# Two blocks of the first adjacency row multiply x and x2 as they arrive, and two chunks of a graph kernel take their blocks in another order

## The reference, cut to what matters

```python
h  = relu(adj @ x @ gcn_w + gcn_b)            # product 1: adj @ x
h  = layernorm(h) * ln_g + ln_b
y  = mamba(h)                                 # conv of 4 taps, silu, a scan over the 4096 rows, gate
x1 = layernorm(x + y)
def conv(v, W, b):                            # products 2 and 3: adj @ x1, adj @ x2
    ax = adj @ v
    t = ax + (1.0 + eps) * ax
    for i in range(3):
        t = relu(t @ W[i].T + b[i])
    return t
out = layernorm(x1 + concat(conv(x1, W1, b1), conv(x2, W2, b2)) @ Wm.T + bm)
```

## Time and profile before

| what | value |
|---|---|
| three executions | 809.51, 811.18, 810.60 us, median 810.6 |
| the profiled execution, its time | 809.39 us |
| its span, first to last instruction | 807.6 us |
| TensorE busy | 792.5 us (98%) |
| VectorE, GpSimd, ScalarE busy | 626.0, 620.3, 437.8 us |
| DMA | 227.42 MB, mean 282 GB/s |
| granted TensorE clock, mean | 0.998 |

### The profile page before, as it was taken

How to read it: one execution, slowest core, us unless ns; L and a number is a source line. 1 busy time by engine, 2 the same in 40 slices (tenths; PEclk the granted TensorE clock), 3 DMA queues, 4 the chain that set the end, 5 groups by cost and what they waited for, 6 DMA issues and landing times.

```text
span 807.6 us, 7621 instructions
## 1 busy us (share of the span) xinstructions
PE 792.5 (98%) x2094; PEld 362.8 (45%) x2094; DVE 626.0 (78%) x881; ACT 437.8 (54%) x822; POOL 620.3 (77%) x300
## 2 busy tenths in 40 slices
PE   7999999999999999999999999999999999999996
PEld 3434444444454444443444444434544454444453
DVE  0146799999898988889899898977988988882136
ACT  0166676477647764766477646662486545321234
POOL 0005899999998989889989998979799899970036
PEclk9999999999999999999999999999999999999999
DMA  9999777777766999998779966899878897887602
GB/s 340 393 367 326 239 225 269 229 254 239 240 226 210 372 375 328 343 375 329 240 254 354 393 244 210 292 329 337 283 248 274 313 338 244 309 295 272 248 26 79
DMA packets 63390, 227.42 MB, mean 282 GB/s; under 512 B 7394, under 2 KB 8180, under 8 KB 44916
## 3 DMA queue, kind: packets, MB, share of 16 engines
q1 hardware_dynamic: 24804, 156.40, 52.0%
q10 hardware_dynamic: 38544, 70.54, 27.5%
HBM read 224.29 MB, written 2.62 MB: 281 GB/s over the span
## 4 chain that ended last, share of the span: by engine, by line
PE 88%; DVE 4%; DMA 3%; ACT 3%; issue 1%; ACTq 0%; DVEq 0%
PE p_x L503 47%; PE p_x L533 16%; PE p_two L533 11%; PE p_m L604 2%; DMA x_s<-x_tiles 2%; PE p_dA L696 2%; PE p_m L620 2%; DMA spread_C<-bc_rows 1%; DVE p_h L980 1%; PE p_two L594 1%; PE p_m L587 1%; PE p_m L624 1%; PE p_two L581 1%; PE p_h L696 1%; PE p_m L616 1%; DVE prod L993 1%
## 5 line engine op out<-in xcount | busy, mean ns | idle before, releaser
L503 PE MATMUL p_x<-ring,x_s 128*128 128x512 f32 x1024 | 455.8, 596 | 2.8 <-DMA x_s<-x_tiles 2.6
L1214 POOL TENSOR_TENSOR bh<-spread,dtu 128x1024 f32<-128x1024 f32 x127 | 299.7, 2360 | 34.2 <-DVE bh L1157 34.2
L1223 POOL TENSOR_TENSOR y<-y,prod 128x1024 f32<-128x1024 f32 x120 | 282.6, 2355 | 54.1 <-DVE prod L993 46.0
L503 PEld LDWEIGHTS p_x<-ring,x_s 128*128 128x128 f32 x1024 | 192.7, 191 | 249.0 <-issue 241.6
L980 DVE TENSOR_TENSOR_SCAN p_h<-p_dA,state,bh 128x512 f32<-128x512 f32 x224 | 276.1, 1278 | 20.7 <-ACT p_dA L706 9.7
L706 ACT ACTIVATE p_dA<-dt,A 128x512 f32<-128x512 f32 x256 | 172.0, 686 | 128.4 <-DVE p_h L980 126.8
L993 DVE TENSOR_TENSOR prod<-p_h,spread_C 128x1024 f32<-128x1024 f32 x120 | 145.7, 1214 | 1.4 <-DMA spread_C<-bc_rows 0.2
L533 PE MATMUL p_x<-ring,x 128*128 128x512 f32 x304 | 137.3, 593 | 0.8 <-ACT acc L939 0.8
L533 PE MATMUL p_two<-ring,x 128*128 128x512 f32 x208 | 94.3, 594 | 2.1 <-DVE dtu L1093 2.0
L533 PEld LDWEIGHTS p_x<-ring,x 128*128 128x128 f32 x304 | 57.1, 190 | 70.8 <-issue 70.8
L424 POOL TENSOR_SCALAR dtu<-prod,mv,rstd 128x128 f32<-128x128 f32 x26 | 20.4, 802 | 63.0 <-ACT rstd L965 63.0
(11 more groups left out here) (133 smaller groups left out, 605.4 us busy)
## 6 DMA issues: line engine op xcount, KB each, us to landing
ring<-adj_blocks SPq DMA_DIRECT2D x143, 1024.0 KB, 7.1
spread_C<-bc_rows ACTq DMA_DIRECT2D x128, 256.0 KB, 5.8
spread<-bc_rows ACTq DMA_DIRECT2D x127, 256.0 KB, 5.1
ring<-adj_blocks SPq DMA_DIRECT2D x8, 256.0 KB, 7.1
x_s<-x_tiles SPq DMA_DIRECT2D x8, 256.0 KB, 10.4
x_s<-x_tiles ACTq DMA_DIRECT2D x7, 256.0 KB, 9.8
out_tiles<-dtu SPq DMA_DIRECT2D x7, 256.0 KB, 2.0
pack<-pack_w ACTq DMA_DIRECT2D x1, 1026.0 KB, 11.8
```

What stands on the lines that cost most here:

```text
L503: return pe.matmul(bank[:, :], tiles[:, JT * m + jt, :], ring[:, i % RING, jt, :], start=opens, stop=closes)
L1214: pool.tensor_tensor(bh[:, i % 3, :, :], both(spread[:, q, :]), dtu[:, c % 2, :, :], ALU.mult).then_inc(s_bmul, 1)
L1223: pool.tensor_tensor(y[:, c % 2, :, :], y[:, c % 2, :, :], prod[:, i % 2, :, :], ALU.add).then_inc(s_acc, 1)
```

## The change

- BOTH = 2: the blocks (0, 0) and (0, 1) multiply x and x2 as they come in the start. The blocks' partial sum for x2 closes in `p_x2`, VectorE copies it to `kept` (a slice of x1's last buffer, unused until chunk 4 is over), and adds it when the rest of row 0 is complete, in a step of its own (`rows_0`) that takes the place of ScalarE's copy of that row. ScalarE's queue brings the first 8 tiles of x2 between those of x. PIECES is 1: only block 0 comes in pieces.
- The two blocks are used for x1 alone later, at the end of chunk 3: eight matmuls of x2 are gone from that chunk and stand in the start.
- In chunk 5 the block (5, 4) comes before the x2 blocks (5, 5) to (5, 7), the sum of row 2 opens after (5, 5), and rows 3 and 4 change places: row 3 now gathers in `p_x` behind row 2, row 4 in `p_two`, last.
- FILL: 11 matmuls instead of 10 stand behind the first gcn and 11 instead of 12 behind the first dt.

```diff
-PIECES = 2
+PIECES = 1
+BOTH = 2
-RAMP = row(X, 0, ALL)
+RAMP = row(ONE, 0, ALL[:BOTH]) + row(X, 0, ALL[BOTH:])
-FILL = {"gcn": 10, "in_x": 7, "x_proj": 3, "dt": 12}
+FILL = {"gcn": 11, "in_x": 7, "x_proj": 3, "dt": 11}
 CHUNK_BLOCKS = [
...
-    row(X, 6, (1,)) + row(X1, 4, (0, 1)) + mixed(row(X, 6, ALL[2:]), row(X2, 0, ALL[3:])) + row(DOUBLE, 0, ALL[:3]),
+    row(X, 6, (1,)) + row(X1, 4, (0, 1)) + mixed(row(X, 6, ALL[2:]), row(X2, 0, ALL[3:])) + row(DOUBLE, 0, (2,))
+    + row(X1, 0, (0, 1)),
...
-    row(DOUBLE, 5, ALL[:4]) + row(X2, 5, (5, 6)) + row(DOUBLE, 5, (4,)) + row(X2, 5, (7,))
-    + row(X1, 2, (2, 3, 4)) + row(X1, 4, (2, 3, 4)) + row(X1, 3, (2, 3, 4)),
+    row(DOUBLE, 5, ALL[:5]) + row(X2, 5, (5,)) + row(X1, 2, (2, 3, 4)) + row(X2, 5, (6, 7))
+    + row(X1, 3, (2, 3, 4)) + row(X1, 4, (2, 3, 4)),
 SUMS = [
...
-        ("x", 5, (0, 1, 2, 3, 4)), ("x", 2, (2, 3, 4)), ("two", 4, (2, 3, 4)), ("x", 3, (2, 3, 4)),
+        ("x", 5, (0, 1, 2, 3, 4)), ("x", 2, (2, 3, 4)), ("x", 3, (2, 3, 4)), ("two", 4, (2, 3, 4)),
...
+        kept = x1[:, KEEP - 1, :, :].rearrange("p t n -> p (t n)")
...
+                if part == "x2" and i < BOTH:
+                    opens, closes = (i, jt) == (0, 0), (i, jt) == (BOTH - 1, JT - 1)
...
+            for jt in range(JT):
+                pe.wait_ge(s_tile[jt], 48 if jt < 2 else 16)
+                block_part(0, jt, jt + 1)
+                block_part(0, JT + jt, JT + jt + 1)
...
+            for jt, tiles in ((0, slice(0, 1)), (1, slice(1, JT))):
+                act.dma_start(x_s[:, tiles, :], x_d[0, :, tiles]).then_inc(s_tile[jt], 16)
+                act.dma_start(x2_s[:, tiles, :], x2_d[0, :, tiles]).then_inc(s_tile[jt], 16)
...
+                elif name == "rows_0":
+                    dve.tensor_tensor(ax2[:, q % 2, :], p_x2[:, :], kept, ALU.add).then_inc(s_ax2, 1)
...
+            dve.wait_ge(s_blk_used, BOTH)
+            dve.tensor_copy(kept, p_x2[:, :]).then_inc(s_kept, 1)
```

More of the change, by code:

```diff
@@ L131, in blocks_with @@
     return [i for i, blk in enumerate(LOADS) if part in blk[0] and blk[1] == n]
-FIRST_OF = {(part, n): blocks_with(part, n)[0] for part in ("x", "x2") for n in range(NC)}
+FIRST_OF = {(part, n): blocks_with(part, n)[BOTH if (part, n) == ("x2", 0) else 0]
+            for part in ("x", "x2") for n in range(NC)}
 LAST_OF = {(part, n): blocks_with(part, n)[-1] for part in ("x", "x2") for n in range(NC)}
@@ L471, in _ @@
                 load(NBLK + k)
+                if k < BOTH:
+                    continue
                 sp_.dma_start(x2_s[:, JT * k:JT * (k + 1), :], x2_d[k]).then_inc(s_x2s[k], 16)
@@ L500, in first @@
                     wait(pe, s_taken, taken)
-                if part == "x2" and jt == 0 and i < FIRST[1]:
+                    if part == "x2" and taken == 0:
+                        pe.wait_ge(s_kept, 1)
+                if part == "x2" and i < BOTH:
+                    opens, closes = (i, jt) == (0, 0), (i, jt) == (BOTH - 1, JT - 1)
+                if part == "x2" and jt == 0 and PIECES <= i < FIRST[1] and m:
                     pe.wait_ge(s_x2s[m], 16)
@@ L631, in _ @@
                 pe.matmul(p_m[:, 0:WARM_W], sq[:, 0:P], sq[:, 0:WARM_W], start=True, stop=True)
-            for k in range(NBLK):
-                if k:
-                    pe.wait_ge(s_xs[k], 16)
-                if k < PIECES:
-                    for jt in range(JT):
-                        pe.wait_ge(s_tile[JT * k + jt], 32 if k == 0 and jt < 2 else 16)
-                        block_part(k, jt, jt + 1)
-                else:
-                    block_part(k, 0, JT)
+            for jt in range(JT):
+                pe.wait_ge(s_tile[jt], 48 if jt < 2 else 16)
+                block_part(0, jt, jt + 1)
+                block_part(0, JT + jt, JT + jt + 1)
+            for k in range(1, NBLK):
+                pe.wait_ge(s_xs[k], 16)
+                block_part(k, 0, len(block_steps(LOADS[k])))
             pe.wait_ge(s_pack, 16)
@@ L945, in _ @@
                             take_x(n)
-                        if rows_complete(n, "x2") == (c, unit):
+                        if n and rows_complete(n, "x2") == (c, unit):
                             take_x2(n)
@@ L1100, in step @@
                     aggregate(s_stats, b).then_inc(s_stats, 1)
+                elif name == "rows_0":
+                    q = X2_ROWS.index(0)
+                    dve.wait_ge(s_px2, 1 + X2_DOUBLE.index(0))
+                    dve.wait_ge(s_mm2, 4 * (q - 2) + 1)
+                    dve.tensor_tensor(ax2[:, q % 2, :], p_x2[:, :], kept, ALU.add).then_inc(s_ax2, 1)
                 elif name == "mlp3":
@@ L1123, in steps_of @@
                     put(min(unit + 1, S - 1), int(unit == S - 1), "mlp3", q)
+                done = rows_complete(0, "x2")
+                if c == done[0]:
+                    put(done[1] + 1, 0, "rows_0", 0)
                 if c + 1 < NC:
```

16 lines of the change are left out of this document (7 added, 9 removed).

## The result

The changed kernel takes **816.4 us** (median of 6 runs, 813.95 to 816.8) for 810.5 us of the kernel before (6 runs, 808.17 to 812.15). The ratio is 1.007, with a 95% interval of 1.0048 to 1.0093: 0.7% slower. The profiled execution took 816.80 us, its span is 815.0 us; before they were 809.39 and 807.6.

A forecast was written before the change was run, and what follows sets the result against it. TensorE, busy 98% of the span, was taken as the bound. Terms +5.8 - 1.0 - 2.2 + 1.9 = +4.5 us gave 815.1 us; the terms' bounds were 812.6 to 818, the range 810.9 to 818.5.

The forecast's parts named there:

- TensorE is the bound, and only its gaps change the time: Whole kernel: TensorE busy 98% of the span, its 768 matmuls stay, all gaps together some 7 us.
- The start: Row 0: 6.9 us of x2 work added, 3.3 us of gaps removed; done at 41.8, +5.8 us (+4.7 to +7.1).
- the nearest neighbour's 7.1 us after issue: Start: landing time of the third DMA (256 KB), taken for the fourth, issued at 2.1, so landing at 9.2.
- The filling: Chunk 0: eleventh matmul fills the 0.5 us before in_x, and the 0.2 us ring wait goes; -1.0 us.
- Chunks 1 and 2: Chunks 0 to 2 move by +4.8 as a whole, the scan with them, locked to TensorE's steps.
- Chunk 3: Eight matmuls and the dtu wait go, 7.9 us, but only -2.2 us is gained (-3.2 to -1.3).
- the scan gains only what it waits for TensorE: Chunk 3: VectorE's waits for out (0.93) and mlp3 (1.64) less rows_0 (0.69) give 1.9 us; with rounding, 1.8.
- the four new waits: Chunk 3: the other 5.7 us become TensorE waits ahead of x_proj, dt, mlp0 and z.
- Chunk 5: New wait for ScalarE's copy against two removed waits, 2.3 us: balance +1.9 us (+1 to +2.5).
- The forecast's wait of 4.2 us: Chunk 5: TensorE waits from 519.73 to 523.9 for ScalarE's copy of row 5's sum, behind table load and decays.
- rival 4: Chunk 5's gap makes the granted clock fall; four matmuls at 1.72 us add 3.4 us, 818.5 us; chance 0.10.
- Rivals 1 to 3: Rival 1 all hidden, 803.3 us (0.10); rival 2 chunk 5 smooth, 810.9 (0.12); rival 3 chunk 3 follows, 809.4 (0.08).

The follow-up runs named there:

- the one with zero weights: Changed kernel with four zero-weight matmuls of 512 columns added where TensorE waits for ScalarE's copy in chunk 5; 814.3 us, ratio 1.0061.
- the two with the reordered start: Changed kernel with row 0's x steps of block 0 ahead of its x2 steps, 817.3 us; the same start together with both moves, 816.4 us.
- both moves: Changed kernel, old chunk 5, reordered start, x2 block moved from chunk 4 to 3, row 5's x1 block from 5 to 4; 816.4 us, ratio 1.0078.

## Why the prediction was right, and where its terms were off

The forecast was 815.1 us (+4.5) with slower as the likeliest; the medians gave 816.4 (+5.9). In the profiles the terms add up to +7.4: three came out larger by 1.1 to 1.4 us and one smaller by 1.1, so part of the agreement is that misses cancelled. (The lower bound that follows from the forecast's terms is 812.1 us, not 812.6.)

- **TensorE is the bound, and only its gaps change the time.** Right: its records are the same in number, and every us of the difference is found as a gap or as records at double spacing.
- **The start, +5.8, measured +6.93** (and +7.0 to +7.6 in the four other kernels with this very start: the upper bound of 7.1 was too low). In the changed kernel the mechanism was right, the second piece waits for the DMA issued fourth. The size was off by its landing: I took the nearest neighbour's 7.1 us after issue, 9.2; it started at 10.25, 8.1 us after the issue at 2.14. That 1.05 us is nearly the whole miss of 1.1. The neighbour came from a kernel in which the second block was in pieces with packets of 2 KB, and here its packets were of 8 KB. In the four other kernels the DMA landed at 9.6 to 10.4, and in two of them (the one with zero weights, the one with a block moved to chunk 3) TensorE didn't wait for it at all: its records still stood 0.85 us apart when it landed, until 11.8 and 10.7, and row 0 was done at +7.63 and +7.04. So the slow beginning was a second mechanism, which the forecast didn't have. The forecast also rested on a wrong reading of the earlier trace rows: I counted 3.3 us of gaps in the old start as time spent waiting for x that work could fill. About 2 us of it were four records at double spacing (1.0, 1.0, 1.0 and 0.85 us apart), which no transfer explains and which the new start has as well.
- **The filling, -1.0, measured -0.86** in the changed kernel; alone in the kernel before it was worth nothing, since the ring's wait and chunk 3 took it back.
- **Chunks 1 and 2, forecast 0, measured +1.35** in this profile: a wait of 0.7 us for ScalarE's copy `ax`, which stood behind a DMA issue of its own, and smaller ones. Of the four other kernels with this very start three show none of it and the one with the old chunk 5 has 1.06, in chunk 2; the two with the reordered start have 1.35 and 0.8. It comes in some executions and not in others, and what decides that stays open.
- **Chunk 3, -2.2 (-3.2 to -1.3), measured -3.3.** The step "the scan gains only what it waits for TensorE" held, and 6.9 us less work made the chunk 3.0 to 4.0 us shorter in five profiles. Mis-sized was what VectorE gains, 3.0 us for 1.8 here. A third wait for TensorE went, 0.30 us ahead of gcn's first step, and one of 0.49 us between a scan and its own copy; and rows_0 made its stretch only 0.4 us longer and not 0.69 (from the scan's start to the copy of its state 2.96 us, for 2.57 at the same place before). The wait for the rows of C gave nothing here (1.41 us for 1.23), but it is what varies most from one profile to the next (0 to 3.6 us), and the range didn't count it. Of the four new waits three came (x_proj 0.86, dt 1.13, z 1.12); the one ahead of mlp0 came in other kernels with the same chunk (2.0 us in the kernel with zero weights in chunk 5, 1.4 us in the one with the old chunk 5). ScalarE's copy at the chunk's end is where TensorE waits, and VectorE's scan is what it waits for.
- **Chunk 5, +1.9, measured +3.3.** The forecast's wait of 4.2 us was 4.0 with the 0.16 us added to its bracket, and without the fall of the clock the term is +1.94 (the run with zero weights): the term was right. What came on top is the mechanism of rival 4, the granted clock, at 1.7 us in this profile, 1.5 in the kernel before with this order, 2.7 with the reordered start. I had taken it for the less likely case (0.10) at +3.4, partly because the column of the granted clock says 1.00 through the gaps of the start; the trace has no record of the clock before 9.08 us (last section), so for the longest of these gaps it was no evidence. The fall came in every profile that had a wait of 3 us or more for a bank in chunk 5 (six of six), and in none of the eight others in that chunk. Elsewhere, the program's last microseconds aside, it came four times, in chunk 3 or at its end, behind waits of 1.13 us (the changed kernel), 1.95 (zero weights), 2.21 (old chunk 5) and 2.63 (both moves). In the changed kernel the clock was back soon: 0.50 over 530 to 532, 0.87 over the next 2 us. Rival 4's 1.72 us for a matmul at the lower level had no row of the kernel before behind it; the runs showed records 0.85 us apart at 0.50, 1.71 us for the two of a matmul, and three to seven such records in each of these falls.
- **Rivals 1 to 3.** Fallen: the parts that they took as free (chunk 5's copy in time, chunk 3 giving 7.9 us) did not come.

By the medians: the old chunk 5 in the changed kernel takes off 3.3 us and leaves 2.7 of start, filling and chunk 3 together.

Open: why the rows of C come late in some executions of chunk 3; whether the start can be made to carry its x2 work at no cost. A start whose adjacency blocks come sooner was not tried.
